# Post-norm attention and RWKV channel mix on eight cores: Q's input without its own load, and the softmax denominator finished in step order

## The reference

```python
q, k, v = (jnp.einsum('bsm,hmd->bhsd', x, kernel[i]) for i in range(3))
attn = jax.nn.softmax(jnp.einsum('bhsd,bhtd->bhst', q, k) / (d*d*h), axis=-1)
out = jnp.einsum('bhst,bhtd->bhsd', attn, v)
out = einsum('bsf,fm->bsm', transpose(out, (0, 2, 3, 1)).reshape(b, s, d*h), WO[0])
x = _layernorm(x + out)
# channel mix, then residual and layer norm
x_prev = x shifted by one token (zero first)
xr = mu_r * x + (1 - mu_r) * x_prev ;  xk = mu_k * x + (1 - mu_k) * x_prev
r = sigmoid(xr @ W_r.T) ;  k = square(relu(xk @ W_k.T))
x = _layernorm(x + r * (k @ W_v.T))
```

## Time and profile before

| | us |
|---|---|
| median of 3 runs | 3061.19 (3004.09 to 3143.18) |
| the profiled execution | 3003.93 |
| its span, core 7, first to last instruction | 3002.0 |
| busy: PE, ACT, DVE | 2163.4, 1250.9, 835.1 |
| matmuls | 10176 |

### The profile page before, as it was taken

The page is one execution under the profiler, slowest core; times in us unless marked ns, Lnnn a source line. Parts: engine busy times, 40 slices in busy tenths (PEclk is TensorE's granted clock), DMA queues, the critical chain, the costliest instruction groups (busy, mean ns, idle before and its releaser), DMA issues.

```text
span 3002.0 us, 30183 instructions; the slowest of 8 cores (2979.6 to 3002.0 us)
## 1 busy us (share of the span) xinstructions
PE 2163.4 (72%) x10176; PEld 727.9 (24%) x10176; DVE 835.1 (28%) x1369; ACT 1250.9 (42%) x1441; POOL 21.9 (1%) x29
## 2 busy tenths in 40 slices
PE   0038688678868886878677778877887788778836
PEld 0013222222222232223233222222322232223212
DVE  0012200240424052405162104032323332232255
ACT  0000177355525653565300364645453556365602
POOL 0000000000000000000000000000000000000000
PEclk9998888788978897889788898877988798879868
DMA  9951300100310032002202203010121012101201
GB/s 173 205 149 21 84 1 1 43 1 29 113 43 1 28 103 52 1 28 88 67 14 31 68 29 104 10 43 1 57 84 43 1 57 84 43 1 57 85 28 56
DMA packets 87215, 159.33 MB, mean 53 GB/s; under 512 B 2016, under 2 KB 18464, under 8 KB 87072
## 3 DMA queue, kind: packets, MB, share of 16 engines
q1 hardware_dynamic: 61968, 123.84, 12.9%
q0 software_dynamic: 25104, 33.56, 7.3%
HBM read 159.51 MB, written 31.46 MB: 64 GB/s over the span
## 4 chain that ended last, share of the span: by engine, by line
PE 51%; ACT 17%; DVE 13%; DMA 12%; issue 6%; ACTq 1%; DVEq 0%; POOL 0%; SPq 0%; POOLq 0%
PE psg L99 26%; ACT pb L109 13%; PE psden L99 9%; PE pspv L99 9%; DMA aba<-xT 6%; DMA ws<-wts 3%; ACT lta L109 3%; PE psa L99 3%; PE psb L99 3%; DVE stv L118 3%; DMA wsc<-ws 2%; DVE recb L118 2%; DVE xka L118 2%; DVE xra L118 2%; DVE outb L118 2%
## 5 line engine op out<-in xcount | busy, mean ns | idle before, releaser
L109 ACT ACTIVATE pb<-psa 128x1024 bf16<-128x1024 f32 x512 | 522.3, 1020 | 519.4 <-PE psa L99 518.4
L109 ACT ACTIVATE pb<-psb 128x1024 bf16<-128x1024 f32 x512 | 523.4, 1022 | 390.9 <-PE psden L99 228.5
L99 PE MATMUL psg<-aba,ws 128*128 128x512 bf16 x992 | 266.6, 423 | 305.2 <-DMA ws<-wsc 188.4
L99 PE MATMUL pspv<-pb,vtb 128*64 128x512 bf16 x2048 | 437.6, 437 | 57.7 <-DVE aba L118 57.7
L99 PE MATMUL psden<-pb,cstb 128*32 128x512 bf16 x2048 | 412.8, 421 | 42.2 <-ACT pb L109 42.2
L99 PE MATMUL psa<-qtb,ktb 64*128 64x512 bf16 x1024 | 216.1, 416 | 167.6 <-ACT pb L109 153.2
L118 DVE TENSOR_TENSOR aba<-pspv,rsb 128x512 bf16<-128x512 f32 x64 | 44.2, 690 | 978.1 <-ACT rsb L109 978.1
L99 PE MATMUL psg<-xra,ws 128*128 128x512 bf16 x960 | 258.9, 425 | 3.0 <-DVE xra L118 1.9
L99 PE MATMUL psb<-qtb,ktb 64*128 64x512 bf16 x1024 | 219.7, 411 | 55.2 <-ACT pb L109 55.2
L99 PEld LDWEIGHTS psg<-aba,ws 128*128 128x128 bf16 x992 | 100.4, 107 | 454.8 <-issue 374.2
L99 PEld LDWEIGHTS pspv<-pb,vtb 128*64 128x64 bf16 x2048 | 111.4, 110 | 327.8 <-issue 327.8
(11 more groups left out here) (99 smaller groups left out, 1551.4 us busy)
## 6 DMA issues: line engine op xcount, KB each, us to landing
ws<-wsc SPq DMA_DIRECT2D x36, 2048.0 KB, 10.1
ws<-wts POOLq DMA_DIRECT2D x8, 2048.0 KB, 25.1
aba<-xT POOLq DMA_DIRECT2D x16, 1024.0 KB, 14.3
y<-xT SPq DMA_DIRECT2D x8, 2048.0 KB, 8.1
outT<-outb SPq DMA_DIRECT2D x32, 512.0 KB, 3.1
wsc<-ws SPq DMA_DIRECT2D x7, 2048.0 KB, 14.7
cstf<-cst SPq DMA_DIRECT2D x1, 96.0 KB, 2.4
cstb<-cst POOLq DMA_DIRECT2D x1, 8.0 KB, 3.5
```

What stands on the lines that cost most here:

```text
L99: i = e.matmul(_o, _l, _r, start=_st, stop=_sp, tile_position=_tp, skip_group_check=True)
L109: i = e.activation(_o, _i, _f, scale=_s, bias=_b)
```

## The change

Three edits of order, one of where data lies; no operation on data is added or taken away, but two of the sixteen 1 MB loads of x are.

- K and V walk over the token blocks in the order 1, 2, 3, 0, so that block 0 is still in `aba` when Q of the first tile is computed; that tile's own load is gone.
- The other tiles' x goes to `xra` in place of `aba`. Its load is emitted on POOL behind the attention of the tile before, where it waits only for that attention's last v pair.
- `early_den_drain` is gone. The last two denominator steps come with their products, in `flush_pv`, and Ln and Exp behind the last of these.
- The fillers of the channel mix of a tile with t > 0 start at step 50, not 42.

```diff
-                for tb in range(NT):
+                for tb in (1, 2, 3, 0):
...
+                    if tb == 0:
+                        kv_nxb0[0] = nxb
...
             def q_group(t, oc, qev, u):
-                xbch = [ABA[:, k * QT:(k + 1) * QT] for k in range(8)]
+                xsrc = ABA if t == 0 else XRA
+                xbch = [xsrc[:, k * QT:(k + 1) * QT] for k in range(8)]
...
-                def early_den_drain():
-                    for i, (hp_, kt_, g_, nd_) in enumerate(pend):
-                        if nd_:
-                            wait("t", c_p, exp_hist[g_])
-                            emit_den(hp_, kt_, g_)
-                            pend[i] = (hp_, kt_, g_, False)
-                    wait("a", c_kt, c_kt.n)
...
                     emit_pv(hp, kt, g)
-                    if nd:
-                        emit_den(hp, kt, g)
+                    emit_den(hp, kt, g)
                     if kt == NKT - 1:
-                        nrc = att["lnd"]
+                        wait("a", c_kt, c_kt.n)
+                        achain_start()
+                        if last_nrb[0]:
+                            wait("a", c_rb, last_nrb[0])
+                        nln = act(LTA[0:64, 0:512], DEN[0:64, :], AF.Ln,
+                                  inc=c_ar)
+                        wait("a", c_ar, nln)
+                        nrc = act(RCR[0:64, :], LTA[0:64, 0:512], AF.Exp,
+                                  scale=-1.0, inc=c_rc)
...
-                        if kt == NKT - 1:
-                            early_den_drain()
...
-                emit_xb(t, prev if (prev is not None and t > 0) else None, u)
+                u["nxb"] = kv_nxb0[0] if t == 0 else xra_nxb[0]
...
-                        steps = [42 + 3 * i for i in range(18)]
+                        steps = [50 + 3 * i for i in range(18)]
...
+                if t < NT - 1:
+                    wait("g", c_xb, c_xb.n)
+                    if prev is not None:
+                        wait("g", c_g, prev["fv_last"])
+                    xra_nxb[0] = dma(
+                        "g",
+                        bass.AP(XRA, 0, [[NCH * QT, 128], [QT, 8], [1, QT]]),
+                        bass.AP(xT, seq * D * S + (t + 1) * QT,
+                                [[S, 128], [128 * S, 8], [1, QT]]), c_xb)
```

More of the change, by code:

```diff
@@ L395, in build_nc @@
             kvf = []
+            kv_nxb0 = [0]
+            xra_nxb = [0]
             if prev is not None:
@@ L801, in emit_pv @@
                        kt_ == NKT - 1, tp=(0, 64))
-                def early_den_drain():
-                    for i, (hp_, kt_, g_, nd_) in enumerate(pend):
-                        if nd_:
-                            wait("t", c_p, exp_hist[g_])
-                            emit_den(hp_, kt_, g_)
-                            pend[i] = (hp_, kt_, g_, False)
-                    wait("a", c_kt, c_kt.n)
[L810 to L820, removed]
                 def flush_pv():
-                    hp, kt, g, nd = pend.pop(0)
+                    hp, kt, g = pend.pop(0)
                     if att["epi"] is not None:
@@ L840, in flush_pv @@
                     emit_pv(hp, kt, g)
-                    if nd:
-                        emit_den(hp, kt, g)
+                    emit_den(hp, kt, g)
                     if kt == NKT - 1:
-                        nrc = att["lnd"]
+                        wait("a", c_kt, c_kt.n)
[7 more added lines that the diff above has]
+                                  scale=-1.0, inc=c_rc)
+                        last_achain[0] = (c_rc, nrc)
+                        bDEN.free = (c_ar, nln)
                         b = next_bank()
@@ L861, in emit_attention @@
                         g = emit_scores_exp(hp, kt)
-                        pend.append((hp, kt, g, True))
+                        pend.append((hp, kt, g))
                         if len(pend) >= 3:
                             flush_pv()
-                        if kt == NKT - 1:
-                            early_den_drain()
                         step[0] += 1
```

## The result

The changed kernel takes 2822.75 us (median of 10 runs), against 3001.85 us (median of 10 runs of the kernel before). The ratio is 0.9404, with a 95% interval of 0.9392 to 0.9415: 179 us or 6.0% less. The forecast was 2832 us, in a range of 2735 to 2915. Comparisons leave out runs in which some cores show a lower clock than the others whatever the kernel; that explains the highest single times of both.

What follows compares the result with a forecast made beforehand. PE was taken to set the pace, with waits at tile starts and head-pair ends and a lowered clock behind them. 34.4 + 53 + 54.5 + 25 + 8 - 2.6 = 172 us off 3003.9 gave 2832 us, range 2735 to 2915.

Steps and rivals of the forecast that it cites:

- Tiles 0 and 4: Start of tiles 0 and 4: x's load goes, Q's first group runs at full clock; 34.4 us gained.
- The six other tiles: Start of tiles 1 to 3 and 5 to 7: the moved load is hidden, DVE is late next; 53 us gained.
- The 4 us that I had deducted: Start of the six other tiles: longer at the low clock after the first scores, 0.7 us a tile; 57 became 53.
- The late load: Rival, six tiles: POOL or its queue holds the load beyond the projection, that term is gone; 2885 us, chance 0.03.
- the case in which DVE isn't in the way: Upper bound for the six tiles' starts: without DVE's operations delaying Q's first cast, 93 us gained, not 53.
- The end of a head pair and the clock: Head pairs' ends: 54.5 us from shorter waits, 25 from the clock (0.5 an end), less 2.6 at tiles' ends.
- 50 x 1.09: Head pairs' ends: 50 of 56 gain 1.09 us each, 54.5 in all; six bound by DVE gain nil.
- The 2.6 us that I took off for the tiles' ends: Last end of each of 8 tiles: last denominator comes one product later, 0.33 us each; 2.6 us lost.
- The shift: Fillers 8 steps later: the second layer norm's DVE work no longer precedes a head pair's product; 8 us gained.
- ends with fillers gain nothing: Rival, head pairs' ends: only 21 ends without fillers gain, 46 us less gain; 2878 us, chance 0.2.
- The clock did not stay up: Rival, head pairs' ends: the clock level may not fall at all, 115 us in place of 25; 2742 us, chance 0.1.
- it always came back: Opposing rival, 21 head pairs without fillers: PE's clock stays low throughout, costing 176 us; 3087 us, chance 0.02.

Runs made afterwards that it cites:

- the combination: Changed kernel with Q's first cast ahead of DVE's 16 operations, ACT's copy behind the third Exp and the token mix in four pieces: 2707.8 us, ratio 0.9053.

## Why the prediction was right

The sum was 172 us, the measurement says 179, and the range held. But two of the terms were far off, and that the total agrees so closely is luck. The terms, one by one:

- **Tiles 0 and 4**, 34.4 us: measured alone, 35. Right.
- **The six other tiles**, 53 us: 60 by the times, 56 by the mean spans. The mechanism is as told: the load hidden, DVE's 16 operations next, 9.6 us of waiting. From a tile's last Exp to the next one's first, the six places took 262.5 us in the mean of the cores and take 208.3, which is 54 us. The 4 us that I had deducted for a longer stretch at the lower clock behind it can't be found: the tiles themselves took 259.7 us and take 259.5 with the loads alone. No run separates this term further. The late load and the case in which DVE isn't in the way are both out.
- **The end of a head pair and the clock**, 54.5 + 25 - 2.6 = 77 us: 47 alone, 49 on top of the loads. This step failed in size. Where no fillers lie it was right, 1.5 us an end for 1.59. The failed part is "50 x 1.09", and with it the 0.5 us for the clock at each of these ends: I took one end in a tile for bound by DVE and had the row for a second in hand, the 1.50 us of the earlier trace rows. Its gain was given back there almost whole (1.06 of 1.09). With two such ends 44 are left; at the 1.4 to 1.5 us seen in tile 0 that would still be over 60. The others among fillers gain less than in tile 0: at step 82 of tile 2, where a filler stands behind the spreading matmul, PE waited 1.72 us in all with the old end (loads alone) and 1.26 with the new, 0.46 less and not 0.9. How the rest of the shortfall is spread over the other ends I didn't work out. The 2.6 us that I took off for the tiles' ends did not show either: with the new end alone the six places between tiles took 260.4 us for 261.5 (cores 0 to 3).
- **The shift**, 8 us: 57 alone, 35 on top of the rest. The second step that failed, and measured alone the larger. I had put down only the 1.50 us of waiting for DVE. I had not seen that a filler due at the end of a head pair covers the wait for the third Exp, and that the statistics, once shifted, do so at one more end; nor that the faster ends make the wait for DVE 2.57.
- **The total** is right because these two errors have opposite signs: 28 us too much in the one, 27 too little in the other, counted on top of the rest. They aren't independent: the three edits alone add up to 95 + 47 + 57 = 199 us and together give 179. I take this to be because the ends and the shift work at the same waits; it is not shown edit by edit.

Of the rivals, "ends with fillers gain nothing" was half right. The clock did not stay up (0.88 in tile 0), and it always came back: in the attention of the profiled core's eight tiles no stretch at the lower level is longer than 20.5 us. The matmuls on unused data show what keeping it up is worth in tile 0: 1.4 us an end, within the bound of 2.3.

## What to carry to other kernels

A filler (independent work put among the steps) is worth most where the main chain waits anyway. Before counting a reordering as "the same work, later", look at which waits its pieces cover at the new place, and which in-order queue they stand in. Where the same engine's queue holds both a long burst and the operation that frees a buffer, any gain ahead of that operation is lost until the burst is cut or moved. And measure edits one at a time even when the total agrees with the forecast: here two terms were off by almost 30 us each, and hid each other.

## What was not expected of the hardware

Adding matmuls made the kernel faster. With nine more at each end of a head pair the granted clock over six head pairs rose from 0.88 to 1.00, and the whole fell by 36 us; in the combination, with seven or three an end, by about 90 us, at a mean clock of 0.94 for 0.90. In the changed kernel the lower level came behind waits of 0.80 and 1.75 us, with the spreading matmul between them: the scores behind the second are busy for 0.61 us and not 0.39. The Trainium skill says of TensorE's clock gate that idle time brings the lower level and activity the higher one (TensorE: Matmul & The Clock Gate, section "Part 1: The HAM clock gate"). The runs agree.

The moved loads landed faster than the six in their old place. The first took 8.5 us, with only casts out of PSUM beside it; the five others took 9.9 to 12.4 us, each beside two casts of `outb` to `rg` and a 2 MB load into `y`. In the old place it was 13.5 to 18.1 us, beside DVE's 16 operations and a 2 MB weight load; the loads of tiles 0 and 4, beside such a weight load and no copy of `outb`, took 14.6 and 14.9 us. The Trainium skill's rule that a DVE copy holds up a DMA on GpSimd's queue (SBUF — State Buffer, section "SBUF: two separate sides") would have the five slower than the first. They are, but the load into `y` is beside them too, and no run here separates the two.
